# Attention stages of a four-layer kernel: query tiles in the order 5 2 4 3 7 0 6 1, value products in four equal parts per group

## What is computed

```python
q, k, v = heads(ln(x) @ Wq), ln(x) @ Wk, ln(x) @ Wv  # 16 query heads of 64, one shared key and value head
q, k = l2norm(q) * q_scale, l2norm(k) * k_scale      # first and third attention layer; second: q / 8
sim = einsum('bhid,bjd->bhij', q, k) * scale + bias  # with one null key in front
sim = where(causal or masked, -big, sim)
x = x + ln(merge(einsum('bhij,bjd->bhid', softmax(sim), v)) @ Wout)
```

## Time and profile before

| | |
|---|---|
| median of three runs | 2574.79 us (2572.8 to 2579.59) |
| the profiled execution | 2561.63 us, its span 2559.9 us |
| TensorE busy, matmuls | 2039.8 us (80% of the span), 42,802 |
| VectorE busy | 1740.8 us (68%) |
| ScalarE busy | 1330.1 us (52%) |
| GpSimd busy | 1037.1 us (41%) |
| granted TensorE clock, mean | 0.797 of full speed |

### The profile page before, as it was taken

How to read it: one execution, slowest core, us unless ns; L and a number is a source line. 1 busy time by engine, 2 the same in 40 slices (tenths; PEclk the granted TensorE clock), 3 DMA queues, 4 the chain that set the end, 5 groups by cost and what they waited for, 6 DMA issues and landing times. The chain is left out here.

```text
span 2559.9 us, 105978 instructions
## 1 busy us (share of the span) xinstructions
PE 2039.8 (80%) x42802; PEld 1640.4 (64%) x42802; DVE 1740.8 (68%) x3900; ACT 1330.1 (52%) x2719; POOL 1037.1 (41%) x1307
## 2 busy tenths in 40 slices
PE   5996868888778877877788788875877888888868
PEld 4885546666666667656666666675545666666658
DVE  4778686677676748566666766648586677766656
ACT  2224556556555643355555655534655566655543
POOL 1442134445545434034445444412134455544432
PEclk8997886777877788966778877777896778767779
DMA  4430665233233322886666766640565333333332
GB/s 145 143 117 1 202 232 148 90 102 95 80 98 102 100 86 89 286 250 193 178 183 188 205 177 192 196 159 17 182 231 157 92 92 101 95 97 90 97 102 99
DMA packets 252477, 351.18 MB, mean 137 GB/s; under 512 B 57447, under 2 KB 134381, under 8 KB 252045
## 3 DMA queue, kind: packets, MB, share of 16 engines
q1 hardware_dynamic: 252044, 344.72, 43.7%
HBM read 256.91 MB, written 104.48 MB: 141 GB/s over the span
## 5 line engine op out<-in xcount | busy, mean ns | idle before, releaser
L1903 POOL TENSOR_SCALAR at_row<-at_row,at_inv 128x129 f32<-128x129 f32 (+7 forms) x384 | 667.7, 1739 | 655.9 <-DVE at_inv L1799 653.8
L1824 DVE CUSTOM_DVE_ANT_0 at_row<-at_s,bias,at_row 128x128 f32<-128x128 f32 (+7 forms) x768 | 608.9, 793 | 469.3 <-PE at_s L1760 426.3
L1848 ACT ACTIVATE at_row<-at_row,at_nmax 128x129 f32<-128x129 f32 (+7 forms) x768 | 593.8, 773 | 545.2 <-DVE at_nmax L1824 544.1
L1759 PE MATMUL at_s<-k_hh,q_hl 128*128 128x512 f32 (+3 forms) x1152 | 541.9, 475 | 158.5 <-DVE at_nmax L1824 105.4
L1760 PE MATMUL at_s<-k_lp,q_h 65*128 65x512 f32 (+3 forms) x1152 | 471.9, 422 | 7.0 <-issue 7.0
L1759 PEld LDWEIGHTS at_s<-k_hh,q_hl 128*128 128x128 f32 x1152 | 268.7, 233 | 319.0 <-DVE at_nmax L1824 188.8
L1772 PE MATMUL at_o<-at_turned,at_v 32*64 32x128 f32 (+3 forms) x18432 | 382.9, 317 | 70.5 <-issue 61.6
L1808 DVE STREAM_TRANSPOSE at_turned<-at_row 128x1024 f32<-128x1024 f32 (+3 forms) x384 | 396.6, 1034 | 52.0 <-PE at_o L1772 42.1
L1772 PEld LDWEIGHTS at_o<-at_turned,at_v 32*64 32x64 f32 x18432 | 338.3, 162 | 123.5 <-issue 102.8
L1760 PEld LDWEIGHTS at_s<-k_lp,q_h 65*128 65x128 f32 x1152 | 279.9, 243 | 32.1 <-issue 7.0
L1843 ACT ACTIVATE at_row<-at_row,at_inv 128x129 f32<-128x129 f32 (+7 forms) x384 | 292.5, 762 | 0.7 <-DVE at_inv L1799 0.7
(11 more groups left out here) (251 smaller groups left out, 3004.2 us busy)
## 6 DMA issues: line engine op xcount, KB each, us to landing
q_hl<-q_dram SPq DMA_DIRECT2D x192, 256.0 KB, 4.3
q_dram<-o_in SPq DMA_DIRECT2D x76, 512.0 KB, 4.0
bias<-bands_dram SPq DMA_DIRECT2D x64, 512.0 KB, 6.4
q_h<-q_dram SPq DMA_DIRECT2D x96, 256.0 KB, 5.1
o_dram<-o_sb SPq DMA_DIRECT2D x96, 256.0 KB, 4.8
bands_dram<-brow_dram SPq DMA_DIRECT2D x2, 8192.0 KB, 30.9
bias<-corners_dram SPq DMA_DIRECT2D x256, 64.0 KB, 4.2
bias<-in_fside SPq DMA_DIRECT2D x32, 448.0 KB, 4.8
```

The lines of the kernel that those rows point to most:

```text
L1759: eng.matmul(out, q_hl[:, g % 2, side, at], t["k_hh"][:, b, c:c + n], start=True, stop=False)
L1824: eng.tensor_tensor_reduce(out=row[:, u % RING, ZERO:ZERO + width], in0=s_ps[u % 2][:, 0:width], in1=bt[:, lo:lo + width], scale=-1.0, sca ...
L1848: eng.activation(cells(u), cells(u), ACT.Exp, scale=-1.0, bias=nmax[:, i:i + 1], accum_out=rsum[:, i:i + 1]).then_inc(s["exp"], 1)
L1903: eng.tensor_scalar(cells(u), cells(u), inv[:, u % RING:u % RING + 1], None, ALU.mult).then_inc(s["norm_p"], 1)
```

## The change

The query tiles of a pair are taken in the order 5 2 4 3 7 0 6 1 (`TILES`). The even group now holds tiles 2 to 5, the odd group 0, 1, 6 and 7. In `turned` and in the query buffer the tiles of a group lie in rising order. Each group's value products run to its widest tile: 24 blocks of 32 keys in the even group and 32 in the odd one, in four equal parts each, at units 0, 2, 4 and 6, with the output copy at unit 7. The odd group's tiles are no longer neighbours, so its query loads and its output stores go in two runs of 256 columns. The ring of weight rows gets slots of the size that each position needs, the buffers `turned` are split by side, one value block moves into the space left in `o_in1`, and TensorE's wait for the value blocks stands ahead of the first products. The ring of bias rows is laid out for the new order, with 12 rows loaded ahead in place of 14. The first query loads of both groups now follow the sixteenth stored product. The diff, cut:

```diff
@@ -30,17 +30,40 @@
...
+TILES = (5, 2, 4, 3, 7, 0, 6, 1)
+GT = NT // 2
...
-HEAD_SLOTS, BIAS_IN_FLIGHT, ROWS_FIRST = 4, 16, 14
+HEAD_SLOTS, BIAS_IN_FLIGHT, ROWS_FIRST = 4, 16, 12
...
 
 
+def tile_of(u):
+
+    return TILES[(u // 2) % NT]
+
+
+def group_tiles(g):
+
+    return sorted(TILES[g % 2 * GT:(g % 2 + 1) * GT])
+
+
+def group_runs(g):
+
+    tiles = group_tiles(g)
+    starts = [n for n, tile in enumerate(tiles) if n == 0 or tile != tiles[n - 1] + 1] + [GT]
+    return [(tiles[a] * P, a * P, (b - a) * P) for a, b in zip(starts, starts[1:])]
+
+
+QUERY_LOADS = [3 * 16 * len(group_runs(g)) for g in range(2)]
+OUTPUT_STORES = [16 * len(group_runs(g)) for g in range(2)]
+
+
 def bias_places():
 
-    widths = [((u // 2) % NT + 1) * P for u in range(4 * NT)]
+    widths = [(tile_of(u) + 1) * P for u in range(4 * NT)]
     places, at = [], 0
     for width in widths:
...
@@ -1209,11 +1232,11 @@
                     low_done(eng, s, q)
                     eng.dma_start(t["q_dram"][b * NPAIR + pair(q), :, :, cols].rearrange("k p i -> p k i"), f32(q_slots[q % NST])
                                   ).then_inc(stored, 16)
-                    if q in (NPAIR - 1, 2 * NPAIR - 1):
-                        g = q // NPAIR
-                        first_of = g * NPAIR
-                        eng.wait_ge(s[f"store{first_of % NST}"], 16 * (first_of // NST + 1))
-                        load_queries(eng, t, s["first"], g, 0)
+                    if q == 2 * NPAIR - 1:
+                        for first_of in (0, NPAIR):
+                            eng.wait_ge(s[f"store{first_of % NST}"], 16 * (first_of // NST + 1))
+                        for g in range(2):
+                            load_queries(eng, t, s["first"], g, 0)
...
@@ -1562,10 +1585,11 @@
 
 def load_queries(eng, t, sem, g, pair):
 
-    cols = slice((g % 2) * BANK, (g % 2 + 1) * BANK)
     one = bass.ds(pair, 1)
     for out, part in ((t["q_hl"][0:DH, g % 2, :, :], 0), (t["q_hl"][DH:P, g % 2, :, :], 1), (t["q_h1"][0:DH, g % 2, :, :], 0)):
-        eng.dma_start(f32(out), t["q_dram"][one, part, :, cols].rearrange("o (s d) i -> d (o s) i", d=DH)).then_inc(sem, 16)
+        for from_, to, n in group_runs(g):
+            eng.dma_start(f32(out[:, :, to:to + n]),
+                          t["q_dram"][one, part, :, from_:from_ + n].rearrange("o (s d) i -> d (o s) i", d=DH)).then_inc(sem, 16)
 
...
@@ -1613,16 +1637,14 @@
     NGRP = U // GU
     TURNS = NPAIR // HP
     RING = 8
-    VALUES_AT = ((1, 4), (0, 2, 4, 6))
-    KEYS_IN_PART = 8
-    OUTPUT_AT = tuple(at[-1] + 1 for at in VALUES_AT)
+    VALUES_AT = (0, 2, 4, 6)
+    OUTPUT_AT = 7
...
@@ -1633,28 +1655,43 @@
...
-        tile = (u // 2) % NT
+        tile = tile_of(u)
         return u % U // (2 * NT), tile, u % 2, (tile + 1) * P
 
     def key_groups(g):
-        return (g % 2 + 1) * GT * QGROUPS
+        return (group_tiles(g)[-1] + 1) * QGROUPS
+
+    def place_of(u):
+        return group_tiles(u // GU).index(unit(u)[1])
+
+    slot_sizes = [ZERO + (max(TILES[i // 2], TILES[GT + i // 2]) + 1) * P for i in range(RING)]
+    slot_at = [sum(slot_sizes[:i]) for i in range(RING)]
 
     with tensors(nc) as (sb, ps):
         q_hl, q_h1, bt = t["q_hl"], t["q_h1"], t["bias"]
         o_sb = t["o_sb"]
-        v_blocks = [sb(f"at_v{n}", [P, NTT, DH])[:] for n in range(B * 2 - 1)] + [t["v"][:]]
-        row = sb("at_row", [P, RING, ZERO + S])
-        turned_late = sb("at_turned", [P, 2, key_groups(1), GT * QG])
-        turned = [t["q_out"][1].rearrange("p (s b i) -> p s b i", s=2, i=GT * QG), turned_late[:]]
+        side_size = key_groups(0) * GT * QG
+        first_side, first_values = t["q_out"][1][:, 0:side_size], t["q_out"][1][:, side_size:]
+        v_blocks = ([first_values.rearrange("p (n d) -> p n d", d=DH)] +
+                    [sb(f"at_v{n}", [P, NTT, DH])[:] for n in range(1, B * 2 - 1)] + [t["v"][:]])
+        row = sb("at_row", [P, sum(slot_sizes)])
+        turned = [[first_side.rearrange("p (b i) -> p b i", i=GT * QG), sb("at_turned0", [P, key_groups(0), GT * QG])[:]],
+                  [sb(f"at_turned1{side}", [P, key_groups(1), GT * QG])[:] for side in range(2)]]
         nmax, rsum, inv = (sb(f"at_{n}", [P, RING]) for n in ("nmax", "rsum", "inv"))
         s_ps = [ps(f"at_s{n}", [P, S]) for n in range(2)]
         o_ps = ps("at_o", [P, QGROUPS, BANK])
 
         def null_cell(u, n=1):
-            return row[:, u % RING:u % RING + n, ZERO - 1]
+            at, size = slot_at[u % RING], slot_sizes[u % RING]
+            return row[:, at:at + n * size].rearrange("p (n c) -> p n c", n=n)[:, :, ZERO - 1]
+
+        def weights(u):
+            at = slot_at[u % RING] + ZERO
+            return row[:, at:at + unit(u)[3]]
 
         def cells(u):
-            return row[:, u % RING, ZERO - 1:ZERO + unit(u)[3]]
+            at = slot_at[u % RING] + ZERO
+            return row[:, at - 1:at + unit(u)[3]]
...
                     place.wait(eng, "out", g + 1)
+                    eng.sem_inc(s["gate"], 1)
                     one = bass.ds(place.turn * HP + (place.half * NPAIR + g // 2), 1)
-                    cols = slice((g % 2) * BANK, (g % 2 + 1) * BANK)
                     last = place.known() and place.half == B - 1 and place.turn == TURNS and g + 2 >= 0
-                    eng.dma_start(t["o_dram"][one, :, cols].rearrange("o p i -> p (o i)"), o_sb[:, g % 2, :]
-                                  ).then_inc(t["o_stored"] if last else s[f"o{g % 2}"], 16)
...
@@ -1749,10 +1789,10 @@
                     p, tile, side, width = unit(u)
                     g = u // GU
                     if u % GU == 0:
-                        turn.wait_loads(eng, f"q{g % 2}", 48 * NGRP // 2, 48 * (g // 2 + 1))
+                        turn.wait_loads(eng, f"q{g % 2}", QUERY_LOADS[g % 2] * NGRP // 2, QUERY_LOADS[g % 2] * (g // 2 + 1))
                     b = turn.half_of(u)
                     turn.wait(eng, "biased", u - 1)
-                    at = slice((tile % 4) * P, (tile % 4 + 1) * P)
+                    at = slice(place_of(u) * P, (place_of(u) + 1) * P)
                     for c in range(0, width, BANK):
...
@@ -1765,14 +1805,15 @@
                     turn.wait(eng, "turned", GU * (g + 1))
                     turn.wait(eng, "out", g)
                     half = turn.half_of(GU * g)
-                    for b in range(part * KEYS_IN_PART, (part + 1) * KEYS_IN_PART):
-                        at = max(0, b // QGROUPS - g % 2 * GT) * QG
+                    keys_in_part = key_groups(g) // len(VALUES_AT)
+                    for b in range(part * keys_in_part, (part + 1) * keys_in_part):
+                        at = sum(tile < b // QGROUPS for tile in group_tiles(g)) * QG
                         for a in range(QGROUPS):
                             for side in range(2):
                                 last = eng.matmul(o_ps[side * DH:(side + 1) * DH, a, at:GT * QG], value_rows(half, b, a),
-                                                  turned[g % 2][a * QG:(a + 1) * QG, side, b, at:GT * QG],
+                                                  turned[g % 2][side][a * QG:(a + 1) * QG, b, at:GT * QG],
                                                   start=b == 0, stop=b == key_groups(g) - 1)
-                    if (part + 1) * KEYS_IN_PART == key_groups(g):
+                    if part == len(VALUES_AT) - 1:
                         last.then_inc(s["pv"], 1)
...
@@ -1780,10 +1821,10 @@
                         logits(turn, n + 3)
                     u = n - LAG
                     g = u // GU - 1
-                    if u % GU in VALUES_AT[g % 2] and has(g, NGRP):
-                        values(turn, g, VALUES_AT[g % 2].index(u % GU))
-                    if turn.known() and turn.half == 0 and turn.turn < 0 and n == U + LATE - 1:
+                    if u == U + GU and turn.known() and turn.half == 0 and turn.turn < 0:
                         eng.wait_ge(s["v_in"], 16 * QGROUPS * len(v_blocks))
+                    if u % GU in VALUES_AT and has(g, NGRP):
+                        values(turn, g, VALUES_AT.index(u % GU))
 
...
@@ -1804,9 +1845,9 @@
                     turn.wait(eng, "pv", u // GU - 1)
                     eng.sem_inc(s["gate"], 1)
                     width = unit(u)[3]
-                    at = (u // 2) % GT * QG
-                    eng.transpose(turned[u // GU % 2][:, u % 2, 0:width // QG, at:at + QG],
-                                  row[:, u % RING, ZERO:ZERO + width].rearrange("p (b i) -> p b i", i=QG)
+                    at = place_of(u) * QG
+                    eng.transpose(turned[u // GU % 2][u % 2][:, 0:width // QG, at:at + QG],
+                                  weights(u).rearrange("p (b i) -> p b i", i=QG)
...
@@ -1871,7 +1912,7 @@
                         normalize_even(turn, n - 1)
                     u = n - LAG
                     g = u // GU - 1
-                    if u % GU == OUTPUT_AT[g % 2] and has(g, NGRP):
```

(1 more changed line is left out.)

32 lines of the change are left out of this document (18 added, 14 removed).

## The result

The changed kernel takes 2596.26 us (median of six, 2585.91 to 2604.22) against 2573.8 us for the one before on the same chip: ratio 1.0088, interval 1.0061 to 1.0115. It is slower by 0.9% where I forecast 2.6% faster. The time lies above the forecast's own range of 2470 to 2550, inside the wide one that takes in the rivals.

What follows compares the result with a forecast made beforehand. TensorE sets the pace: by its work and instruction stream with wide tiles, by the chain logits, bias, logits with narrow ones. 58+19+26-84-39-50+3 = -67 us, from 2574.8 to 2508 us; own range 2470 to 2550, with rivals 2425 to 2635.

Steps and rivals of the forecast that it cites:

- (f): Granted clock in the attention stages: fewer entries into the low level save 50 us (0 to 130).
- (c): TensorE's instruction fetch before value products: 6,144 more at 4.3 ns each cost 26 us (0 to 157).
- (a): Value products on TensorE: 896 a pair in place of 768 cost 58 us of busy time (30 to 99).
- (b): TensorE's turns between products and logits: eight parts a pair in place of six cost 19 us (10 to 40).
- (d): TensorE's waits for VectorE before logits, 105.4 us: a fifth stays, saving 84 us (40 to 105).
- (e): Logits that start on an empty array after a wait: four fifths of 48 us go, saving 39 us (15 to 50).
- (g): Split query loads and output stores, bias rows queued behind them, other waits: 3 us more (0 to 25).
- The instruction stream is the bound: Rival, chance 0.20: product fetch stalls rise to 6 ns each, no clock gain; 57 us slower, 2632 us.
- f is 0: Step of the instruction-stream rival: every fetch hole ends at the low clock, so the clock gain of 50 us is nothing.
- The waits change place: Rival, chance 0.10: VectorE waits for products, then is late for logits; gains halve, 19 us slower, 2594 us.
- Clock up: Rival, chance 0.20: fetch stalls alone no longer pull the clock down, worth 130 us; 147 us faster, 2428 us.
- the one on stage two's bias: Sign of failure: DMA waits before stage two's bias would show that (g) failed; no size given.

## Why the prediction was wrong, step by step

My sum was -67 us, the stages measured +35.5: a miss of 102 us by the two traces, 90 by the medians. Two steps failed: the clock, (f), which was sized far too large, and the fetch stalls, which I priced in (c) only before products and put at nothing before logits, where the loop jumps back.

(a), (b) *More products, more turns*: +77 forecast for both; the products' busy time rose by 71.8 us, of which 12.5 lie over logits. Right in size. (c) *Instruction fetch before products*: +26 forecast, +30.6 measured. The kernel with fewer products gives a + c 79 to 83 us for my 84. But that (c) came out is in part luck. Four parts in place of two took 36 us of these stalls away at the same number of products (157.5 to 121.2), and the added products brought 52 (136.3 to 188.1), some 8 ns each where I had 4.3. At 36,864 products the runs show from 103 to 162 us, so a constant price per instruction is not what they show. That the bursts of bias bands make most of the stalls fell with the narrow bands.

(d) *Waits for VectorE*: -84 forecast, -75.4 before logits and -7.8 before products measured. Right. (e) *Logits on an empty array*: -39 forecast; the logits' busy time fell by 25.1 us, with a slightly better clock in it.

(f) *The clock*, -50 forecast: this step failed. The stages went from 0.756 to 0.770, so the low level holds 798 us in place of 830. By the part of 1.99 or 3.71 us that is 32 x (1 - 1.99 / 3.71) = 15 us at most, about 7 with my half. The low stretches behind narrow tiles did vanish, as I said, and in the changed kernel every fall of the clock that I find in the first stage comes behind a fetch stall. But those that are left last longer: in the first stage 23 low stretches of 10.5 us on average in place of 29 of 8.0, in all three 71 of 10.6 in place of 81 of 9.5. I had counted entries and kept their length. The column experiments show what moves the length: with at most 64 columns there are 50 low stretches of 23.6 us, with mostly 128 there are 59 of 6.2, and the change turns products of 128 columns into products of 64. That this is why its low stretches are longer fits, but no run shows it by itself. Nor does a higher clock that is bought with columns pay: at 0.87, with 39% more columns, the kernel took the same time.

*The missing term.* I priced fetch stalls inside the products and left out those before logits, which were 31.6 us before, and never asked where the loop jumps. They rose by 38.8 us, 29.6 of them at the jumps. What lengthened the jump's stall is the change's first part of the even group, moved from unit 1 to unit 0, into the last step ahead of the jump: kernels with that part there stall for 2.9 to 5.7 us a jump, whatever their order and width (four parts in rising order, in alternating order, the change), those with parts at 1 and 4, two steps free of products, for 1.6 to 2 on average, and the one with a single free step for 3.2. Writing the loop out gave the changed kernel's stages 34 us more than those of the kernel before, which fits 29.6 us of stalls and the low clock behind them. How the part lengthens the stall can be read from the packets of the instruction queue. The last one before the logits behind the jump starts 3.2 us before them on average in both kernels (single ones 2.7 to 4.0 and 2.5 to 3.9 us). When it starts, TensorE has another 1.6 us of work on average in the kernel before, and in the changed one it has been idle for 0.8 us. With one free step it has been idle for 0.1 us, with four parts in rising order for 0.6, and with two parts in the alternating order it has 1.0 us of work. So the fetch is as long in both and less of it is covered, if that packet is TensorE's; the trace does not name the engine that a packet is for. Why it starts later against TensorE's work behind a part of products, no run shows. Of the step that is moved I had counted the products but not what it is moved next to.

(g) *The rest*, +3 forecast: the wait for queries is 14.2 us more (15.4 against 1.2), all in the second stage, where bias rows share the queue. The split loads of 128 KB land in 7.7 us where the whole ones of 256 KB take 4.1, which I had not foreseen; but with the loads in one run the wait is still 10.2 us, so the splitting is about a third and the rest stays open. VectorE's wait for bias rows there grew as well (7.5 us before, 23.5 after), beside TensorE's work.

In one line: busy time came 46 us above the sum (43 of it f, by the estimate of 7), idle time 56 us (39 issue before logits, 30 of that the jumps; 11 more than forecast for the queries).

*The rivals.* "The instruction stream is the bound" had the right sign and nearly the right mechanism, but not its place: the price per product stayed at 188.1 / 43,008 = 4.4 ns, under the 4.7 from which it decides, and the new holes were before the logits. Its step "f is 0" is nearly what happened. "The waits change place" forecast 2594 us, next to the 2596 measured, for a wrong reason: the waits for VectorE did not come back. "Clock up" is out. Of my signs, the packets (408), the matmuls, the waits for VectorE (30.0 us, at the limit of 30) and issue in the products (180 to 190) came right, the clock near 0.80 and the pair at 34 us on average did not (1737.2 / 48 = 36.2); I had named no sign for stalls before logits. Of the signs of failure the one on stage two's bias came true.

## What to carry to other kernels

Price small matmuls by their number and the clock at which they run, not by their columns: 17% more of them cost some 80 us here, 39% more columns cost nothing that could be measured. Ask of a balancing change whether the order within a group gives the gain without any added instruction: here the order with four parts did, 2.4% faster in place of 0.9% slower. In an engine with tens of thousands of instructions keep heavy parts away from the steps ahead of its backward jump, or write the loop out (1.1% in the kernel before, 2.8% in the changed one). Ask of a step that is moved what it is moved next to. When you count on a higher clock, count how long the low stretches last as well as how often they begin.

## What the runs showed of the hardware

TensorE's stalls of over 1 us that end in "issue" end 1.2 to 2.4 us after a packet of 16 KB of instructions has landed (91 of 91 in the changed kernel). A backward jump stalled TensorE for 2.8 to 5.7 us with 64 or 96 small products in the step ahead of it, for 2.7 to 4.0 us with 96 products and then one free step, and for 0.3 to 4.4 us, 1.6 on average, with two free steps; the written-out loop has no stall there and moved 381 packets in place of 408. The granted clock moved with the columns of the products and not with idle time alone: 0.64 with at most 64 columns, 0.77 with the mixture, 0.87 with mostly 128, at the same number of matmuls, and the stretches at the low level lasted 23.6, 10.6 and 6.2 us. The kernel with the lowest clock even has the least idle time in its stages (1764.4 - 1505.3 = 259 us, against 311 and 310). Cutting columns under 128 made the kernel slower (1.0215 in place of 1.0088), because the low clock reached the logits too.
